# A fused attention and mixture-of-experts layer: operands moved by 32 bytes, transposed activations loaded one stage earlier, and routing one group ahead throughout

## What is computed

```
xn  = layernorm(x)                                   # no scale, no bias
qkv = xn @ W_qkv                                     # 256 -> 3 * 256
att = softmax(causal(q @ k.T / 16)) @ v              # one head of width 256
sha = (silu(xn @ sg) * (xn @ su)) @ sd               # shared FFN, 256 -> 512 -> 256
e   = argmax(xn @ gate_w);  s = sigmoid(max(xn @ gate_w))     # top 1 of 32 experts
rou = (silu(xs @ rg[e]) * (xs @ ru[e])) @ rd[e],  xs = xn * s # tokens grouped by expert
out = x + att + sha + rou
```

## Time and profile before

| | us |
|---|---|
| median of 3 runs | 2436.29 (2432.5 to 2442.11) |
| the profiled execution | 2433.08 |
| its span, from the first to the last instruction | 2431.3 |
| PE (matmul) busy | 2347.1, 97% |
| DVE, ACT, POOL busy | 1530.0, 1246.7, 1173.1 |
| mean granted TensorE clock | 0.985 of 2.4 GHz |
| bytes moved | 439.25 MB, mean 181 GB/s |

### The profile page before, as it was taken

The page is one execution under the profiler, slowest core; times in us unless marked ns, Lnnn a source line. Parts: engine busy times, 40 slices in busy tenths (PEclk is TensorE's granted clock), DMA queues, the critical chain, the costliest instruction groups (busy, mean ns, idle before and its releaser), DMA issues. The chain is left out here.

```text
span 2431.3 us, 48912 instructions
## 1 busy us (share of the span) xinstructions
PE 2347.1 (97%) x16118; PEld 2162.2 (89%) x16118; DVE 1530.0 (63%) x3290; ACT 1246.7 (51%) x2286; POOL 1173.1 (48%) x1159
## 2 busy tenths in 40 slices
PE   6999998999989999999999996899999999999997
PEld 6888887888879999999999994698989888888887
DVE  6666666666756777777777771555464555555554
ACT  4444443444435555555555551455555555555554
POOL 2233333333323333433433430677777777777777
PEclk9999999999989999999999998999999999999999
DMA  5555545555547667666666766235444444445441
GB/s 200 195 194 188 183 176 204 177 181 181 187 141 232 225 226 239 230 225 235 233 226 231 240 226 217 87 116 168 138 150 133 157 139 144 150 146 176 143 129 58
DMA packets 302492, 439.25 MB, mean 181 GB/s; under 512 B 36480, under 2 KB 210304, under 8 KB 302336
## 3 DMA queue, kind: packets, MB, share of 16 engines
q1 hardware_dynamic: 284224, 398.91, 48.1%
q0 software_dynamic: 18112, 38.37, 5.5%
HBM read 288.21 MB, written 148.96 MB: 180 GB/s over the span
## 5 line engine op out<-in xcount | busy, mean ns | idle before, releaser
L1223 POOL TENSOR_TENSOR t_p_lo<-t_score,t_p_hi 128x512 fp32r<-128x512 f32 (+1 forms) x320 | 357.5, 1133 | 154.3 <-ACT t_score L1326 116.1
L887 POOL DMA_INDIRECT ahead_rows<-xs_rows,ahead_slot x160 | 197.4, 1234 | 407.6 <-DMA ahead_slot<-token_of 264.7
L1318 ACT COPY t_score<-t_psS 128x512 f32<-128x512 f32 (+1 forms) x320 | 167.2, 522 | 339.4 <-PE t_psS L71 232.8
L1398 PE MATMUL t_psO<-t_v_hi,t_p_hi 128*128 128x258 f32 x1088 | 319.6, 294 | 13.6 <-POOL t_p_lo L1223 13.0
L1400 PE MATMUL t_psO<-t_v_hi,t_p_lo 128*128 128x258 f32 x1088 | 308.8, 284 | 0.0
L1402 PE MATMUL t_psO<-t_v_lo,t_p_hi 128*128 128x256 f32 x1088 | 307.5, 283 | 0.0
L1263 DVE TENSOR_TENSOR t_top<-t_top,t_psS 128x512 f32<-128x512 f32 (+3 forms) x264 | 155.1, 588 | 173.7 <-ACT t_score L1318 170.0
L297 POOL DMA_INDIRECT token_of<-a_token_i,a_slot_i x128 | 140.6, 1098 | 237.0 <-DVE a_slot_i L407 207.7
L69 PE MATMUL t_psS<-t_q_hi,ahead_x_hi 128*128 128x512 f32 (+3 forms) x640 | 235.1, 367 | 6.5 <-DVE t_q_lo L1245 4.0
L70 PE MATMUL t_psS<-t_q_hi,ahead_x_lo 128*128 128x512 f32 (+3 forms) x640 | 234.8, 367 | 0.0
L71 PE MATMUL t_psS<-t_q_lo,ahead_x_hi 128*128 128x512 f32 (+3 forms) x640 | 234.8, 367 | 0.0
(11 more groups left out here) (188 smaller groups left out, 7411.9 us busy)
## 6 DMA issues: line engine op xcount, KB each, us to landing
ahead_raw<-in_L_ffn_routed_gate_w SPq DMA_DIRECT2D x42, 512.0 KB
ahead_raw<-in_L_ffn_routed_up_w SPq DMA_DIRECT2D x42, 512.0 KB
ahead_raw<-in_L_ffn_routed_down_w SPq DMA_DIRECT2D x41, 512.0 KB, 4.8
e_raw<-in_L_ffn_routed_gate_w SPq DMA_DIRECT2D x41, 512.0 KB
e_raw<-in_L_ffn_routed_up_w SPq DMA_DIRECT2D x41, 512.0 KB
e_raw<-in_L_ffn_routed_down_w SPq DMA_DIRECT2D x41, 512.0 KB, 4.5
routed_rows<-e_dout SPq DMA_DIRECT2D x80, 256.0 KB, 4.1
a_xt<-in_L_attn_x SPq DMA_DIRECT2D x32, 512.0 KB, 6.0
```

Of the source, the lines that this page charges most:

```text
L887: g.indirect_dma_start(out=xg[:, k, h], out_offset=None, in_=xs, in_offset=bass.IndirectOffsetOnAxis(slot[:, k, h:h + 1], 0)).then_inc(x_i ...
L1223: g_.tensor_tensor(p_lo[:, t % LR, c0:], score[:, t % SR, c0:], p_hi[:, t % HR, c0:].bitcast(F32), ALU.subtract).then_inc(lo_ok, 1)
L1318: s.copy(score[:, t % SR, c0:], psS[:, n % BANKS, c0:]).then_inc(u_act, 1)
L1398: nc.tensor.matmul(psO[:, a, 0:W], p_hi[:, kp, cols], v_hi[:, kv, j % J], start=j == 0, stop=False, skip_group_check=True)
```

## The change

It has four parts. `TWICE` is empty, so each step from 0 to 30 carries one front, step 30 that of group 31, and step 31 none; group 31 is ranked in step 31. The work that hangs on its rank moves: `tile_tables` into step 31 ahead of `mul(31, 2)`, PE's transposes of the table behind `up(31, 3)`, positions 0 and 1 behind `h_low(31, 2)`, `tile_rows` behind `mul(31, 3)`, and the other six positions to the end. The ten x^T loads leave the end of SP's expert stage and go into its first four steps, two each and four in the first, after the down weights. Unused tiles of 32 bytes ("gap") are laid between others. After it, `ahead_x_hi` and `ahead_x_lo` start on multiples of 64, the shared gate and up weights and `t_q_hi` too, `dw_hi` and `dw_lo` 32 past one, h in the token stage on one, the expert weights on one, and the expert stage's x and h 32 past one.

```diff
-    TWICE = (16,)
+    TWICE = ()
...
-        w_hi = [sb("gw_hi", [P, C, F], F32R), sb("uw_hi", [P, C, F], F32R), sb("dw_hi", [P, IT, D], F32R)]
-        w_lo = [sb("gw_lo", [P, C, F], F32R), sb("uw_lo", [P, C, F], F32R), sb("dw_lo", [P, IT, D], F32R)]
+        sb("gap", [P, 8])
+        up_hi = [sb(f"{n}w_hi", [P, C, F], F32R) for n in "gu"]
+        up_lo = [sb(f"{n}w_lo", [P, C, F], F32R) for n in "gu"]
+        sb("gap0", [P, 8])
+        w_hi = up_hi + [sb("dw_hi", [P, IT, D], F32R)]
+        w_lo = up_lo + [sb("dw_lo", [P, IT, D], F32R)]
+        sb("gap1", [P, 8])
...
                 h_low(i, 1)
+                if i == NG - 1:
+                    tile_tables()
                 mul(i, 2)
                 if before is not None:
                     score_of(before)
+                h_low(i, 2)
                 if i == NG - 1:
-                    tile_rows()
                     positions(0)
                     positions(1)
-                h_low(i, 2)
...
-                if i == NG - 1:
-                    positions(2)
-                    positions(3)
-                    positions(4)
...
                     mul(i, 3)
+                    if i == NG - 1:
+                        tile_rows()
...
-                if i == NG - 2:
-                    tile_tables()
                 if i == NG - 1:
-                    for n in range(5, 8):
+                    for n in range(2, 8):
                         positions(n)
...
+                up(i, 2)
+                if fronts:
+                    values(g, 0)
+                up(i, 3)
                 if i == NG - 1:
                     pe.wait_ge(table_ok, 1)
                     nc.tensor.transpose(psE[:, 0], tile_of[:, 0:1], keep.ident[:])
                     nc.tensor.transpose(psE[:, 1], tile_of[:, 1:2], keep.ident[:]).then_inc(table_mm, 1)
-                up(i, 2)
-                if fronts:
-                    values(g, 0)
-                up(i, 3)
...
         raw = [ahead.raw, sb("raw1", [P, 3, C * F])]
+        sb("gap0", [P, 8])
         whi = [sb(f"whi{k}", [P, 3, C * F], F32R) for k in range(2)]
         wlo = [sb(f"wlo{k}", [P, 3, C * F], F32R) for k in range(2)]
+        sb("gap1", [P, 8])
...
+            def load_transposed(g):
+                sp.dma_start(ahead.x_hi[:, g].bitcast(F32), xth_g[g]).then_inc(ahead.x_in[g], 16)
+                sp.dma_start(ahead.x_lo[:, g].bitcast(F32), xtl_g[g]).then_inc(ahead.x_in[g], 16)
+
+            assert ahead.x_hi.shape[1] == 5
...
                 load_down(t + 2, k)
+                if isinstance(t, int):
+                    load_transposed(t)
+                if is_first(t):
+                    load_transposed(4)
                 if not is_first(t):
                     store(t - 1, 1 - k)
             R = tiles(sp, step)
-            for g in range(ahead.x_hi.shape[1]):
-                sp.dma_start(ahead.x_hi[:, g].bitcast(F32), xth_g[g]).then_inc(ahead.x_in[g], 16)
-                sp.dma_start(ahead.x_lo[:, g].bitcast(F32), xtl_g[g]).then_inc(ahead.x_in[g], 16)
             store(R * 2 + 1, 1)
...
         x_hi, x_lo = ahead.x_hi, ahead.x_lo
+        sb("gap", [P, 8])
         q_hi = sb("q_hi", [P, QR, C, GT], F32R)
...
         C, H = D // P, ST // P
+        sb("gap", [P, 8])
         self.x_hi = sb("x_hi", [P, XR, C, GT], F32R)
```

## The result

The changed kernel takes 2419.24 us (median of four runs, 2417.27 to 2420.83) beside 2436.49 of the kernel before: ratio 0.9926, 95% interval 0.9908 to 0.9945. That is faster by 0.7%, about half of the 33.4 us that the prediction summed up. Its profiled execution took 2420.69 us, span 2418.9.

What follows compares the result with a forecast made beforehand. The prediction took TensorE as the bound in all three stages; its terms, -11.15 + 4 - 10.3 + 3 - 18.9 = -33.4 us, against a median of 2436.3 gave 2403 us, range 2355 to 2430.

Steps and rivals of the forecast that it cites:

- Part 1: Token stage: removing the double step, step 16 with two fronts, gives -11.15 us, bounds -10 and -12.
- Part 2: Token stage's end: later table and slot loads move the border to the experts by +4 us, bounds +2 and +8.
- Part 3: Border to attention: the last store no longer queues behind the x^T loads, -10.3 us, bounds -8 and -12.
- Part 4: Expert stage's first four steps: the early x^T loads make slot lists late, +3 us, bounds 0 and +8.
- Part 5: Matmul spacing: 32-byte placement gives -12.4 us for 256 columns, -6.5 for 512, together -18.9; bounds -56 and +21.
- Rival B: Matmuls of all stages: the placement does nothing, only the other four parts count, 2422 us; chance 0.22.

Runs made afterwards that it cites:

- e3: The kernel before with one front per step, the table and positions moved as in the change, nothing else; 2432.98 us, ratio 0.9984.
- e2: The kernel before with only the x^T loads moved into the expert stage's first four steps; 2433.46 us, ratio 0.9992.
- e5: The changed kernel with the ten x^T loads back at the expert stage's end, issued after the last store; 2415.64 us, ratio 0.9914.
- e12: As e10, but four x^T loads go early, one in each of the first four expert steps, and six behind the last store; 2400.08 us, ratio 0.9857.
- e10: The changed kernel with the x^T loads behind the last expert store and POOL's rows in their planned steps; 2398.13 us, ratio 0.9844.
- e1: The kernel before with all the gap tiles of the change and nothing else; 2423.15 us, ratio 0.9936.
- e7: The kernel before with one 32-byte gap ahead of the expert stage's x and h; 2426.99 us, ratio 0.997.
- e8: The kernel before with four gaps so that x^T alone moves by 32 bytes against all it meets; 2435.11 us, ratio 0.9992.

## Why the prediction was right in sign and half in size

**Part 1, right.** The double step was put at -11.15 us; counted from the first step, step 31 starts 11.6 us sooner in e3 and 10.4 in after, where each step lasts 21.21 us instead of 21.19.

**Part 2, right in mechanism, 2 us too small.** All the moves came at their forecast times, to a microsecond; the border took +6.1 (e3: +5.7), inside the bounds of 2 and 8. What it waits for in its last 7.1 us the profile does not show, and no run settled it. With part 1 the single steps bring 4 us net.

**Part 3, right, 3 us too small.** The store landed and the barrier was through 2.4 us after the issue; I had taken the median of stores that share the queue (4.1 us) and 1 us for the barrier, but this one had the queue to itself.

**Part 4, mis-sized: +3 was put, about +10 measured**, at the far bound of 8 or beyond (the loads alone: +7.6 in e2, 11.0 between e5 and after). The prediction said that slot list 3 lies behind 2.1 MB, 6.5 us, of which PE's lead takes a part. It does: PE stood 4.3 us for that list. But a later list, behind the loads of the fourth step, cost a second wait of 2.7 us, for which nothing had been put; together the waits for gathered rows rose by 6.2 us, and the colder clock around each wait is left for the rest. The bound should have held the clock as well. e12 shows what the queue could carry: two fifths of the volume cost 0.8 to 1.8 us beside e10 and e5.

**Part 5, right where the experts are, wrong elsewhere.** Forecast -12.4 for 256 columns: e1 shows -15.7 over the experts (a tile 9.07 to 8.88 us), and the shared down-projection, counted in with 2.6, gave nothing. Forecast -6.5 for 512 columns: -1.8, in attention alone; gate/up did not follow. I had taken one number of columns for one behaviour, and the 235 ns read for gate/up from one step were 2 to 3 too many: over all of them before has 232.1 and 233.2. With about -17 the term as a whole is near its forecast, but by luck: the experts' gate and up gained 3.2 ns where 1.7 was put, and that made up for the shared projections, which gained nothing. Rival B, the placement is worth nothing, is refuted for the experts. So is what I drew for it from the two-port rule of the Trainium skill's page "TensorE: Matmul & The Clock Gate", What happens when you issue a matmul: independent ports may be so, but the spacing does depend on where the operands lie, 120.0 against 116.8 ns.

**What had no term: the start of attention, +7.9 us.** The prediction went on from PE's share of the stage and the border's time, and looked at no other engine behind the border. There POOL and DVE stood within a microsecond of a collision, in the kernel before as well: 0.96 us apart where 0.7 is needed. A shift of DVE's instruction against POOL's work by half a microsecond decides about 8 us, and e1, e2, e5, e7 and e8, quite different edits, all have it. That the runs without a profile behave alike is not shown; but of ten runs of e8 eight lie from 2432.16 to 2436.41 and two at 2425.45 and 2427.52, and the means of these groups are 8.7 us apart.

In sum the forecast was -33.4 and the span shows -12.4 (the medians -17.3). Of the difference of 21 us, 7.9 are this start of attention, 7.9 the first tiles, 6.5 the token stage's spacing and the end of the double step, 2.1 the border of part 2, and 1.7 the rest of attention; 5.1 came back in the other tiles and at the border of part 3.

## What to carry to other kernels

When a transfer is moved off a border, its volume must be set against what the queue can carry in one step of the place where it goes: 0.5 MB beside 2.1 MB a tile hid, 1 to 2 MB did not, and the order of the store and the loads alone gave over half the gain for free. Where a stage starts, read every engine's timeline for its first 80 us, not PE's alone: a list of work clipped to step 0 was worth 14 to 16 us, nearly as much as the whole change. And a change that shifts one engine by a microsecond can be judged only by its own stretch, with such collisions taken out of the sum.

## What the hardware showed that I had not expected

- A DVE instruction with both inputs in SBUF that takes 0.70 us takes 4.56 to 4.88 when a gather of POOL is under way at its start and a row of three reading instructions follows the gather 0.23 to 0.56 us after that start; POOL's own are not slowed (3.71 us for three, and 3.77 beside ACT), and ACT's four, in the same place, take 1.27. Without a gather under way it is POOL's instruction that waits: 1.22 us instead of 0.74, and DVE's stays at 0.69.
- The distance between matmuls of four-byte operands depends on where the operands start: 120.0 ns to 118.0 for 256 columns when the experts' x moves by 32 bytes, and 116.8 with the change's whole layout, though the experts' weights, x and h lie at the same offsets within 64 bytes in both. What gives the last 1.2 ns, and why the shared projections do not follow, stays open.
- Ten issues on SP's queue took 5.4 us of SP's time in e5, six took 3.1 us in e12. In both SP starts the attention stage 1.2 us behind the last of them, so the stage's end waited for the issues, not for the data.
